# Other steps for the side work of a fused attention and feed-forward block, layer norm outputs on GpSimd, and a max pass with uneven steps

## The reference

```python
def reference(x, w_qkv, b_qkv, w_proj, b_proj, k0, k1, k2, s0, s1, s2):   # x: 16 x 512 x 128, float32
    def attn(x):                                # 16 heads of 8, causal
        q, k, v = split(x @ w_qkv + b_qkv, 3)   # each reshaped to heads
        scores = where(causal, q @ k.T / sqrt(8), lowest)
        a = softmax(scores)
        # heads 0, 1, 2: rows of a times 1.6 in one third of the keys, then normalised again
        return concat_heads(a @ v) @ w_proj + b_proj
    def ffn(x):                                 # w(k) = +1 where k is true, else -1
        h = relu(s0 * (concat([x, -x]) @ w(k0))) * 2        # 256 -> 512
        h = relu(s1 * (h @ w(k1))) * 2                      # 512 -> 512
        return s2 * (h @ w(k2))                             # 512 -> 128
    x = layernorm(x + attn(x))
    return layernorm(x + ffn(x))
```

## Time and profile before

| | |
|---|---|
| median of 3 timed runs | 1007.99 us (995.96 to 1011.67) |
| the profiled execution, its own time | 994.16 us |
| its span, from the first to the last instruction | 992.4 us |
| mean granted clock of TensorE | 0.928 of full speed |
| PE busy | 864.0 us, 87% |
| DVE busy | 671.9 us, 68% |
| ACT busy | 605.0 us, 61% |
| POOL busy | 502.6 us, 51% |

### The profile page before, as it was taken

One profiled execution on the slowest core, in us unless ns is written; L12 is line 12 of the kernel. 1 busy time (PEld: TensorE's weight loads), 2 busy tenths in 40 slices (PEclk: granted clock), 3 DMA queues, 4 the chain that ended last, 5 costly groups with the idle time before them and its releaser, 6 DMA issues.

```text
span 992.4 us, 17320 instructions
## 1 busy us (share of the span) xinstructions
PE 864.0 (87%) x5824; PEld 439.0 (44%) x5824; DVE 671.9 (68%) x2784; ACT 605.0 (61%) x1106; POOL 502.6 (51%) x625
## 2 busy tenths in 40 slices
PE   2349698999999899989999998989999898999866
PEld 1114244545454454545454453545455454535343
DVE  3367578575867768595967669595857769694234
ACT  2106467566766667576757667576756767576733
POOL 1103145637564654647574664646565655547540
PEclk8558899979999997999999799999989999999887
DMA  3653635345453534455443435455443425300000
GB/s 77 68 76 60 71 51 69 45 71 56 52 63 46 74 45 66 53 71 60 53 63 45 66 45 75 49 71 59 57 54 50 70 34 73 38 23 2 23 11 11
DMA packets 66142, 53.19 MB, mean 54 GB/s; under 512 B 4518, under 2 KB 64006, under 8 KB 66054
## 3 DMA queue, kind: packets, MB, share of 16 engines
q1 hardware_dynamic: 65190, 51.30, 40.2%
q10 hardware_dynamic: 864, 0.79, 0.3%
HBM read 9.24 MB, written 4.19 MB: 14 GB/s over the span
## 4 chain that ended last, share of the span: by engine, by line
PE 51%; DVE 23%; POOL 9%; ACT 5%; DMA 5%; issue 4%; SPq 2%; ACTq 1%; POOLq 0%; DVEq 0%
PE av_ps L882 10%; DVE max_ps L643 10%; PE max_ps L825 10%; PE score_ps L849 8%; PE bank_ps L909 5%; POOL h_lo L432 5%; PE bank_ps L910 5%; PE bank_ps L808 4%; PE bank_ps L955 3%; DMA stack<-rowmaxT 3%; DVE stats L712 3%; POOL h_hi L430 2%; DMA stack<-parts 2%; DVE rowmax L643 2%; PE bank_ps L944 2%
## 5 line engine op out<-in xcount | busy, mean ns | idle before, releaser
L643 DVE CUSTOM_DVE_ANT_0 max_ps<-max_ps,future 128x512 f32<-128x512 f32 (+3 forms) x1024 | 480.3, 514 | 232.7 <-PE max_ps L825 229.6
L516 ACT ACTIVATE e<-score_ps 128x512 f32<-128x512 f32 x640 | 365.1, 595 | 187.7 <-PE score_ps L849 184.5
L825 PE MATMUL max_ps<-stack 72*128 72x512 bf16 (+3 forms) x1024 | 260.5, 318 | 59.9 <-DVE rowmax L643 36.1
L849 PE MATMUL score_ps<-stack 75*128 75x512 bf16 (+3 forms) x1024 | 253.8, 310 | 20.8 <-DMA stack<-rowmaxT 16.1
L423 POOL TENSOR_SCALAR_AFFINE_SELECT e<-e 128x512 f32<-128x512 f32 x256 | 160.2, 646 | 129.7 <-ACT e L516 129.7
L882 PE MATMUL av_ps<-e,vaug 128*9 128x512 f32 (+3 forms) x2048 | 194.3, 453 | 3.1 <-ACT avT L523 1.7
L825 PEld LDWEIGHTS max_ps<-stack 72*128 72x128 bf16 x1024 | 83.5, 101 | 218.0 <-DVE rowmax L643 98.3
L432 POOL TENSOR_TENSOR h_lo<-full,h_hi 128x512 fp32r<-128x512 f32 x120 | 153.4, 1278 | 10.0
L508 ACT ACTIVATE full<-bank_ps,scales 128x512 f32<-128x512 f32 x128 | 86.8, 687 | 114.3 <-PE bank_ps L910 93.1
L643 DVE DVE_READ_ACCUMULATOR2_ANT rowmax<- 128x1 f32 x1024 | 143.2, 140 | 0.0
L849 PEld LDWEIGHTS score_ps<-stack 75*128 75x128 bf16 x1024 | 90.1, 100 | 78.7 <-issue 23.8
(11 more groups left out here) (83 smaller groups left out, 791.6 us busy)
## 6 DMA issues: line engine op xcount, KB each, us to landing
stack<-parts SPq DMA_DIRECT2D x288, 128.0 KB
x_in<-in_L_attn_hidden_states SPq DMA_DIRECT2D x16, 256.0 KB, 5.7
x_res<-in_L_attn_hidden_states SPq DMA_DIRECT2D x16, 256.0 KB, 11.4
out_x<-res SPq DMA_DIRECT2D x16, 256.0 KB, 10.9
stack<-rowmaxT ACTq DMA_DIRECT2D x32, 24.0 KB
e<-in_L_ffn_k SPq DMA_DIRECT2D x1, 256.0 KB, 3.5
wc<-in_L_attn_c_attn_w SPq DMA_DIRECT2D x1, 192.0 KB
e<-in_L_ffn_k SPq DMA_DIRECT2D x1, 128.0 KB, 3.3
```

The source lines that it names most:

```text
L516: nc.scalar.activation(e[g % 2][:, t, :], score_ps[:, t % 2, :], ACT.Exp, scale=SCALE).then_inc(exped, 1)
L643: return nc.vector.tensor_tensor_reduce(out=scored_block, in0=scored_block, in1=future[:, P * (T - 1 - qt):S], scale=1.0, scalar=NEG, op0= ...
L825: return nc.tensor.matmul(out_ap[:, col:col + width], st[0:QK_ROWS, h, 0, P * qt:P * qt + P], st[0:QK_ROWS, h, 1, 0:width], start=True, st ...
L849: return nc.tensor.matmul(out_ap[:, col:col + width], st[0:ALL_ROWS, h, 1, P * kt:P * kt + P], st[0:ALL_ROWS, h, 0, P * kt:S], start=True, ...
```

## The change

It moves the side stages to other steps and what hangs on them. PE's step of each, before and now (a result is taken in the same step or up to two later):

| stage | before | now |
|---|---|---|
| xT, q, k | (0,9), (1,0), (1,1) | (0,0), (0,3), (0,4) |
| v | (0,7) | (0,7) |
| tok_0, tok_1, rowmax1, tok_2, tok_3 | (1,2), (1,3), (1,4), (1,5), (1,6) | (1,0), (1,2), (1,3), (1,4), (1,5) |
| attnT, proj | (2,3), (2,6) | (1,7), (1,9) |
| x1T, ffn0_0 to ffn0_3 | (3,2), (3,5), (3,5), (3,8), (3,9) | (2,6), (2,8), (2,9), (3,0), (3,1) |
| rowmax0 | (3,3) | (3,3) |
| ffn1_0 to ffn1_3 | (0,4), (0,4), (0,6), (0,9) | (3,6), (3,8), (0,0), (0,2) |
| ffn2T, ffn2 | (1,8), (2,2) | (0,5), (0,9) |

- The feed-forward of a batch starts earlier: x1T at (2,6), ffn0 from (2,8), ffn1_0 and ffn1_1 in group 3 of the same iteration, ffn1_2, ffn1_3, ffn2T and ffn2 in group 0 of the next.
- xT is at (0,0), q and k at (0,3) and (0,4); xT has two buffers, so that v of an earlier batch need not have read it.
- `max_steps` replaces `ahead`: the max pass does two pieces at (0,1), (0,3) and (0,5) and none at (2,1), (2,2) and (2,7), so that it is up to three pieces ahead in between.
- `normalise_tokens` on POOL applies the layer norms, four tensor_scalar of 128x128 each, in place of ACT's `layernorm_out`. The statistics of the layer norms have steps of their own (LN_STATS).
- The high parts of ffn0_2 and ffn0_3 are made by DVE; hi_ready becomes two semaphores.
- On SP the load of x_res waits for the bank of rowmax0, and the store stands behind it; w_qkv is loaded in two pieces.

```diff
 PLACES = (
...
-    ("ffn1_1", -2, (0, 4), (0, 4)),
...
+    ("ffn1_1", -1, (3, 8), (3, 9)),
...
+HIGH_ON_POOL = ("ffn0_0", "ffn0_1", "ffn1_0", "ffn1_1", "ffn1_2", "ffn1_3")
...
+NEGMAX_SPLIT = (((3, 0), (3, 0), (3, 1), (3, 2)), ((0, 9), (1, 0), (1, 1), (1, 2)))
+
+NEGMAX_ROWS = ((3, 5), (1, 4))
+
+LN_STATS = ((2, 1), (3, 5))
+LN_VAR = ((2, 2), (3, 6))
+
+MAX_TWICE = ((0, 1), (0, 3), (0, 5))
+MAX_NONE = ((2, 1), (2, 2), (2, 7))
...
@@ -179,7 +183,7 @@
         stack = [sb(f"stack{i}", [P, H, 2, S], BF16) for i in range(2)]
         x_in = sb("x_in", [P, T, D])
         x_res = sb("x_res", [P, T, D])
-        xT = sb("xT", [P, S])
+        xT = [sb(f"xT{i}", [P, S]) for i in range(2)]
         qk = sb("qk", [P, 2, S])
         parts = [sb(f"parts{i}", [P, 6, S], BF16) for i in range(2)]
         vaug = [sb(f"vaug{i}", [P, T, H, R + 1]) for i in range(2)]
...
@@ -260,9 +266,19 @@
         def wait_free(eng, u):
             eng.wait_ge(bank_free[u[0]], u[1])
 
-        def ahead(n, g):
-
-            return (n, 3) if g == 0 else (n + 1, g + -1)
+        def max_steps(n, g, t):
+
+            each = [2 if (g_, t_) in MAX_TWICE else 0 if (g_, t_) in MAX_NONE else 1
+                    for g_ in range(G) for t_ in range(STEPS)]
+            first = sum(each[:STEPS * g + t])
+            for i in range(first, first + each[STEPS * g + t]):
+                quarter = i // STEPS
+                b = n + 1 if quarter else n
+                if live(b):
+                    yield b, (quarter + 3) % G, i % STEPS
+
+        highs_of_dve = [w for w in HIGH_STEPS if w not in HIGH_ON_POOL]
+        HIGHS_OF_DVE = len(highs_of_dve)
...
@@ -276,7 +292,8 @@
         @block.sync
         def _(sp):
             sp.dma_start(x_in[:], x_tok[0]).then_inc(x_loaded, 16)
-            sp.dma_start(wc[:], w_qkv).then_inc(w_loaded, 16)
+            sp.dma_start(wqk_in, w_qkv[:, 0:2 * D]).then_inc(w_loaded, 16)
+            sp.dma_start(wv[:], w_qkv[:, 2 * D:3 * D]).then_inc(w_loaded, 16)
...
@@ -350,12 +367,14 @@
                     wait_full(sp, use_of(b + -1, "xT"))
                     sp.dma_start(x_in[:], x_tok[b.times(1)]).then_inc(x_loaded, 16)
                 earlier_half(n)
-                if live(n + -2):
-                    store(n + -2)
+                if live(n + 1):
+                    wait_free(sp, use_of(n + 1, "rowmax0"))
                 if live(n):
                     if n.c > 0:
                         wait_free(sp, use_of(n + -1, "proj"))
                     sp.dma_start(x_res[:], x_tok[n.times(1)]).then_inc(xres_loaded, 16)
+                if live(n + -2):
+                    store(n + -2)
...
@@ -425,24 +443,35 @@
                 last.then_inc(masked, 1)
 
             def high_and_low_part(b, layer, m):
-                k = 1 + FT * layer + m
-                wait_free(pool, use_of(b, f"ffn{layer}_{m}"))
-                nc.gpsimd.tensor_copy(h_hi[layer][:, m, :], full[:, full_slot(b, k), :]).then_inc(hi_ready, 1)
-                pool.wait_ge(hi_ready, b.times(9, k + 1))
-                nc.gpsimd.tensor_tensor(h_lo[layer][:, m, :], full[:, full_slot(b, k), :],
-                                        h_hi[layer][:, m, :].bitcast(F32), ALU.subtract).then_inc(split_ready, 1)
-
-            def rstd_of(b, i):
+                what, k = f"ffn{layer}_{m}", 1 + FT * layer + m
+                hi, whole = h_hi[layer][:, m, :], full[:, full_slot(b, k), :]
+                if what in HIGH_ON_POOL:
+                    wait_free(pool, use_of(b, what))
+                    nc.gpsimd.tensor_copy(hi, whole).then_inc(hi_by_pool, 1)
+                    per = len(HIGH_ON_POOL)
+                    pool.wait_ge(hi_by_pool, b.times(per, HIGH_ON_POOL.index(what) + 1))
+                else:
+                    pool.wait_ge(hi_by_dve, b.times(HIGHS_OF_DVE, highs_of_dve.index(what) + 1))
+                nc.gpsimd.tensor_tensor(h_lo[layer][:, m, :], whole, hi.bitcast(F32),
+                                        ALU.subtract).then_inc(split_ready, 1)
+
+            def normalise_tokens(b, i):
                 pool.wait_ge(ln_step[i], b.times(4, 3))
                 nc.gpsimd.tensor_tensor(rstd[:, i, :], var_eps[:, i, :], minus_half[:],
                                         ALU.pow).then_inc(rstd_ready[i], 1)
                 pool.wait_ge(rstd_ready[i], b.times(2, 1))
                 nc.gpsimd.tensor_tensor(shift[:, i, :], neg_mean[:, i, :], rstd[:, i, :],
                                         ALU.mult).then_inc(rstd_ready[i], 1)
+                pool.wait_ge(rstd_ready[i], b.times(2, 2))
+                x = res2 if i else res1
+                for t in range(T):
+                    ins = nc.gpsimd.tensor_scalar(x[:, t, :], x[:, t, :], rstd[:, i, t:t + 1], shift[:, i, t:t + 1],
+                                                  ALU.mult, ALU.add)
+                ins.then_inc(ln_step[i], 1)
 
             def iteration(n):
                 def low(layer, m):
-                    b = n + (-2 if layer else -1)
+                    b = n + (-2 if layer and m else -1)
...
@@ -526,15 +555,6 @@
                 if b.c * 9 + k >= 2:
                     act.wait_ge(split_ready, b.times(9, k - 1))
                 take(use_of(b, what), full[:, full_slot(b, k), :], func, **kw)
-
-            def layernorm_out(b, i, t, src, dst):
-
-                if t == 0:
-                    act.wait_ge(rstd_ready[i], b.times(2, 2))
-                ins = nc.scalar.activation(dst[:, t, :], src[:, t, :], ACT.Identity,
-                                           scale=rstd[:, i, t:t + 1], bias=shift[:, i, t:t + 1])
-                if t == T - 1:
-                    ins.then_inc(ln_step[i], 1)
 
             def rowmax_rows(b, half):
 
...
@@ -568,9 +583,9 @@
                             if what[:4] == "ffn1":
                                 activation_out(b, 5 + int(what[5]), what, ACT.Relu, scale=scales2[:, 1:2])
                             if what == "xT":
-                                if live(n + 1):
-                                    wait_full(act, use_of(n + 1, "v"))
-                                take(use_of(b, what), xT[:], ACT.Copy)
+                                if live(b + -2):
+                                    wait_full(act, use_of(b + -2, "v"))
+                                take(use_of(b, what), xT[b.parity][:], ACT.Copy)
                             if what in ("q", "k"):
                                 i = "qk".index(what)
...
@@ -724,20 +739,20 @@
 
             def high_part(b, k, hi, what):
                 wait_free(dve, use_of(b, what))
-                nc.vector.tensor_copy(hi, full[:, full_slot(b, k), :]).then_inc(hi_ready, 1)
+                nc.vector.tensor_copy(hi, full[:, full_slot(b, k), :]).then_inc(hi_by_dve, 1)
 
             def low_part(b, k, hi, lo):
 
-                dve.wait_ge(hi_ready, b.times(9, k + 1))
+                done = k if last_batch(b) else 0
+                dve.wait_ge(hi_by_dve, b.times(HIGHS_OF_DVE, done + 1))
                 nc.vector.tensor_tensor(lo, full[:, full_slot(b, k), :], hi.bitcast(F32),
                                         ALU.subtract).then_inc(split_ready, 1)
 
             def iteration(n):
                 for g in range(G):
                     for t in range(STEPS):
-                        b, quarter = ahead(n, g)
-                        if live(b):
-                            take_max(b, quarter, t)
+                        for b, quarter, step in max_steps(n, g, t):
+                            take_max(b, quarter, step)
                         for what, d, _, step in PLACES:
...
@@ -772,16 +785,22 @@
                             if what == "x1T":
                                 high_part(b, 0, x1_hi[:], what)
                                 low_part(b, 0, x1_hi[:], x1_lo[:])
-                            elif last_batch(b):
+                            else:
                                 layer, m = int(what[3]), int(what[5])
                                 k = 1 + FT * layer + m
-                                high_part(b, k, h_hi[layer][:, m, :], what)
-                                low_part(b, k, h_hi[layer][:, m, :], h_lo[layer][:, m, :])
+                                if last_batch(b) or what not in HIGH_ON_POOL:
+                                    high_part(b, k, h_hi[layer][:, m, :], what)
+                                if last_batch(b):
+                                    low_part(b, k, h_hi[layer][:, m, :], h_lo[layer][:, m, :])
                         for k in range(4):
                             if (g, t) == NEGMAX_SPLIT[0][k] and live(n + 1):
                                 split_rowmax(n + 1, 0, k)
                             if (g, t) == NEGMAX_SPLIT[1][k] and live(n):
                                 split_rowmax(n, 1, k)
+                        if (g, t) == LN_STATS[0] and live(n + -1):
+                            layernorm_stats(n + -1, 0, res1)
+                        if (g, t) == LN_STATS[1] and live(n + -2):
```

(1 more changed line is left out.)

126 lines of the change are left out of this document (57 added, 69 removed).

## The result

The changed kernel takes 1029.4 us (median of 4 runs, 1026.3 to 1034.2) against 1004.9 for the kernel before in the same comparison: ratio **1.027, 95% interval 1.021 to 1.033**. It is slower. The profiled execution took 1034.24 us (span 1032.4) against 994.16 (span 992.4); so the two traces differ by 40 us, more than the medians (24.5), because the trace of before is of an execution faster than any in the comparison and that of the changed kernel is of its slowest. In all that follows medians are of every execution, and ratios leave out those that took over 1.5% more than the fastest of their kernel.

The account below looks back on a forecast made before the run. PE was taken as the bound, busy 51.23 of 54.90 us. From the profiled execution, 994.2 + 11 (iterations) - 8 (start) - 6 (tail) = 991 us, ratio 0.997; against the median 1007.99 the forecast is 1006 us, range 972 to 1034.

Parts of the forecast that it names:

- Added: who is late next: Five places in an iteration where PE would newly wait, 4.2 to 6.5 us in sum, 3.4 to 5.7 as idle.
- Start: -8: Batch 0's second rowmaxT load would be through before the first max step waits, saving 8 us (4 to 11).
- What bounds the kernel: PE bounds the iteration, busy 51.23 of 54.90 us; its idle 3.7 us is what can be won inside.
- what the change does to PE's own work: nothing: PE issues the same matmuls, so everything the change does is a count of waits.
- Removed: the gap at (3,0): PE's idle of 2.1 us there goes; the other 1.6 us of idle go or turn into the added waits.
- clock rival: Gaps become too small to pull the clock down: 12.5 us back, 977 us, ratio 0.97; chance 0.28.
- I take +0.8: Chosen cost per iteration within -0.3 to +2.0 us, giving +11 us over the 14 iterations with all their work.
- TENSOR_SCALAR at 0.3 us: Price of each of POOL's four 128x128 layer norm operations before x1T, bounded by 0.2 and 0.32 us.
- the rule: GpSimd about 2x slower than VectorE: the four would take 1.8 instead of 1.2 us, +7 us in all.
- Tail: -6: Without batch 14's ffn2T and ffn2 ahead of attnT, and with two ffn1 tiles moved, 3 to 9 us saved.
- the late rowmaxT load: Rival: rowmaxT's first-half load comes too late for PE at (0,0), 2.6 us per iteration, 1042 us; chance 0.17.
- The collision of DVE and POOL: Rival: splits at (1,0) to (1,3) slowed by POOL, +2.0 us per iteration, 1022 us, ratio 1.014; chance 0.12.

Follow-up runs that it names:

- a2: Changed kernel with tok_0 at (1,1), tok_2 at (1,3) and rowmax1 at (1,4), so one step later for tok_0 and rowmax1: 1025.2 us, ratio to before 1.020.
- c3: Kernel before with the uneven max pass alone, other steps left out than in the change: 978.2 us, ratio to before 0.981.
- a3: Changed kernel with the four layer norm outputs back on ACT, at (2,4) and (3,8): 1029.7 us, ratio to before 1.024.
- a1: Changed kernel with POOL making the masks of (2,7) ahead of the lows of ffn0_0 and ffn0_1: 1028.9 us, ratio to before 1.024.
- a4: Changed kernel with ffn1_2 and its high one step later, at (0,1) and (0,2): 1032.6 us, ratio to before 1.029.
- c2: Changed kernel with the edits of a2 and a4 together: 1029.1 us, ratio to before 1.028.
- d2: Changed kernel with the edits of a1, a2 and a4, the layer norm left on GpSimd: 1012.2 us, ratio to before 1.011.
- b2: Also called all four: changed kernel with the edits of a1, a2, a3 and a4 together: 1006.4 us, ratio to before 1.003.
- d3: The kernel of b2 with proj at (1,8) and res1, its statistics, variance and layer norm one step sooner: 997.5 us, ratio to before 0.997.
- b1: Changed kernel with x1T at (2,7) and the ffn0 tiles one step later: 1059.1 us, ratio to before 1.058.
- c1: The kernel of b2 with x1T and ffn0 one step later: 1046.6 us, ratio to before 1.047.
- b4: Kernel before with the layer norm outputs written by GpSimd in place of ACT: 1007.1 us, ratio to before 1.004.
- d1: Kernel before with the uneven max pass and the layer norm outputs on GpSimd, at its old places: 980.9 us, ratio to before 0.981.
- b3: Changed kernel with a1, a2, a4, x1T and ffn0 later, and batch 2's first-half stack loads held at the start: 1050.8 us, ratio to before 1.041.

## Why the prediction was wrong

Forecast: 1006 us (its own sum, a ratio of 0.997 of 1007.99, gives 1005), within 2% of before; measured 1029.4 us, ratio 1.027. The time lies in the range 972 to 1034, the side was wrong.

Two steps failed. The walk in "Added: who is late next" left out one wait, that of tok_0 for ACT's copy of av, 1.29 us, and put the iteration at +0.8 us where it measured +2.0 at full clock and +2.2 with the falls (a2, which moves tok_0 and rowmax1 later, only exchanged their waits for smaller ones). And "Start: -8" had the wrong load and the wrong sign, +11.6 us at v of batch 2. In the terms of the sum, from one profiled execution each:

| term | forecast us | measured us |
|---|---|---|
| start, to v of batch 2 | -8 | +11.6 |
| iterations, from v of batch 2 to v of batch 15 | +11 | +30.6 |
| tail, from v of batch 15 | -6 | -2.1 |

- **"What bounds the kernel" and "what the change does to PE's own work: nothing"** held: same matmuls, and what changed was waits and the clock.
- **"Removed: the gap at (3,0)"** held, and c3 shows it alone. It is worth more than its idle: the clock falls behind it went too, 1.85 us per iteration in all. My clock rival priced this well (12.5 us back over the run); I didn't see that the added waits would bring the falls back.
- **"Added: who is late next"**: all five places appeared. Measured against the prices in brackets: rowmax1 0.98 (1.2 to 2.7), x1T 1.41 (0.6 to 1.0), ffn0_0 0.71 (0.5 to 0.9), the sums of (3,3) 1.17 (1.0), the bank of ffn1_1 0.88 (0.9). Their sum is 5.15, within the 3.4 to 5.7. **The sixth was missed**: tok_0 at (1,0) needs ACT's copy of av, which ACT makes behind the last exp and the moved copy of qk, 1.29 us. I had walked through DVE's work at (1,0) and not through ACT's. By the text's own subtraction the five make +1.5 us (5.15 against 3.7 of idle) and all six +2.8, yet the iteration at full clock is 2.0 longer: PE's busy time fell from 51.23 to 50.44 us, so that setting idle against idle overstated the loss by 0.8. That the iteration stands right at my upper bound is therefore chance.
- **"I take +0.8"** failed. The full-clock iteration is 2.0 longer, my upper bound. The reason given for the middle, that the bound "has every collision in it", doesn't hold, since a missed place made it up.
- **TENSOR_SCALAR at 0.3 us** was mis-sized: 0.454 each, above the bound of 0.32, and 1.74 for four. The bound came from one-input and two-input operations of another shape. The doubling of DVE's 0.22, which the rule weighed in the prediction (the Trainium skill, GPSIMD Engine Reference, Performance versus the Vector engine) led to, gave 1.8 and was the better price. It decided little: a3, without it, waits 0.15 us less at x1T.
- **The clock.** The text named "if the number of clock falls changes" as what would make it wrong, but carried only the case in which they vanish. They went from every third iteration to nine of ten. Of the 22.4 us in the ten, 20 are the 2.0 of the full-clock iteration, and the rest is the falls' surplus (9 x 1.1 now, 3 x 2.5 before). In size this is the small part; but it is why a1 and a4 didn't move the time. The surplus is small because the slow clock hides two of the six waits.
- **"Start: -8"** failed twice. The load was misnamed, and with it the reason: batch 1's first-half load is issued in group 3 of iteration 0 whatever stands before the first max step. And the start got longer: 7.9 us at v of batch 1, 11.6 at batch 2, 18.6 at batch 3, 20.1 at batch 4. Beyond batch 2 this holds the waits of the iterations too, so that the two errors are about equal, some 20 us each. Between the v of batches 2 and 3, ffn1_3 and ffn2T of batch 0 now stand ahead of v, 16 matmuls more; they account for some 3.7 us (an estimate, 16 starts at 0.23), slow clock for part of the same stretch. With tok and rowmax1 one step later v of batch 4 is at 248.2 to 251.6 in a2, c2, d2, all four and d3, against 254.8 to 259.5 in the changed kernel, a1, a3, a4 and b1, 239.4 before and 240.6 in c3; but c1, with that edit too, has 255.8. Each is a single execution, and the rest of these 9 us or more wasn't taken apart.
- **"Tail: -6"**: from the last v to the end 139.3 us against 141.4, so -2.1. What is late there now is POOL, with lows, the layer norm and masks in one chain (PE waits 10.6 us for POOL behind the last v, 0.4 before).
- **Rivals**: the late rowmaxT load didn't happen (PE's last wait for such a load is the one at 125.02, and x_res lands 3.0 us after its issue). The collision of DVE and POOL did (1.28 and 0.82 us), and its rival's +2.0 per iteration is what the full-clock iteration measured; but that is luck, since PE paid 0.98 us for it, less than the forecast's own price, and a2, which takes most of that away, won 0.06 at full clock on top of a4. The chances as stated don't follow quite from their parts (a tenth of 0.43 on either side gives 0.32, 0.46 and 0.21), which changes nothing here.

Open stays why a fall follows in some iterations and not in others behind the same wait (b2, b4), why three executions of b2 with a higher mean clock were no shorter, and how much of the start is the places and how much the order of SP.

## What to carry to other kernels

Walk through a new order with every engine that supplies a step, not only the busiest: the missed wait of 1.29 us came from ACT, busy 54% of the span. Before taking a wait away, look whether it stands in most iterations: a1 was aimed at one that nine of ten didn't have. Where the clock falls behind gaps, judge an edit by an iteration at full clock and by the clock apart: four edits changed the time by 0.6% or less alone and by 2.4% together, and d3, whose full-clock iteration is 0.6 us longer, is 0.6% faster, with no slow clock in its ten. Try the parts of a bundle apart: here one part held a gain of 1.9% that the others spent.

## What the runs showed of the hardware

- Slow clock hides waits. In the changed kernel a stretch of some 7 us at the lower level made an iteration 1.1 us longer, not 3.5, since two waits behind it (0.71 and 1.17 us) no longer occurred.
- Iterations with slow clock kept their length over several kernels: about 58.02 us in most of those of the changed kernel, a1, a2 and a3, and pairs of 57.0 and 59.0 in a4 and c2. In a4 and c2 slow clock took what the waits lost.
- Neither the largest wait nor the idle time in sum tells how often the clock falls. Largest wait in most iterations, and iterations of the ten with slow clock: d3 0.71, none (one wait of 1.02 among them); d1 0.77, none (one of 1.08); c3 0.95, two; b2 1.26, six; before 1.36, three; b4 1.36, nine; the changed kernel 1.41, nine; c2 1.41, ten; d2 1.41, eight; b3 1.76, six. The three with the smallest have few or none, and among the others there is no order. As to idle time, PE idles 4.5 us per iteration in d3, without falls, and 3.7 before. This is a row of kernels, not a test of the wait alone.
- GpSimd's TENSOR_SCALAR with a pointer per partition for each of two operands took 454 ns for 128x128 f32 and 1.74 us for four; in a3 ACT's ACTIVATE with scale and bias took 482 ns and 1.65 us for four.
- A load of 24 KB issued behind nine 128 KB loads, with a 256 KB load and nine more of 128 KB following, landed in 9.96 us, with all of these held back in 2.69; the nine, issued together with the next nine, then took 16.66.
